# A Flamingo-style block on Trainium2: query projection moved into the cross attention stage, output bias on GpSimd, tanh kept in PSUM, one layer norm as a stage of its own

## What is computed

```
x = x + tanh(g_xattn[l]) * attention_l(layernorm(x), ctx)    # 16 heads of 16; 112 queries, 375 keys
x = x + tanh(g_ffn[l])   * ffn_l(layernorm(x))
```

```
h = gelu(x @ Wi + bi) * sigmoid(x @ Wg + bg);  r = x + h @ Wo + bo;  layernorm(r) * gamma + beta
```

## Time and profile before

| | |
|---|---|
| time, median of 2 runs | 3081.41 us (3079.08 to 3083.74) |
| the profiled execution | 3072.57 us |
| its span, first to last instruction | 3070.7 us |
| busy: PE, DVE, ACT, POOL | 85%, 60%, 44%, 34% of the span |
| mean granted PE clock | 0.917 of full |

### The profile page before, as it was taken

How to read it: one execution, slowest core, us unless ns; L and a number is a source line. 1 busy time by engine, 2 the same in 40 slices (tenths; PEclk the granted TensorE clock), 3 DMA queues, 4 the chain that set the end, 5 groups by cost and what they waited for, 6 DMA issues and landing times. The chain is left out here.

```text
span 3070.7 us, 57383 instructions
## 1 busy us (share of the span) xinstructions
PE 2604.8 (85%) x21112; PEld 2028.9 (66%) x21112; DVE 1848.1 (60%) x3903; ACT 1360.1 (44%) x2680; POOL 1057.2 (34%) x1305
## 2 busy tenths in 40 slices
PE   7998599986998999869599897977768994999995
PEld 7998387874876666546277563554445873888884
DVE  5555687136864333258478346678648865676775
ACT  4444466234662111247366423344334662455552
POOL 3433201022011232257412232453341113677772
PEclk9999699986998999989699998988987995999998
DMA  8888655327640000161655200000035723555553
GB/s 226 248 243 241 175 166 146 128 72 190 175 142 16 1 1 1 44 168 38 166 151 172 83 1 1 1 1 0 1 111 154 187 77 124 197 203 201 187 195 105
DMA packets 153095, 363.52 MB, mean 118 GB/s; under 512 B 26496, under 2 KB 110336, under 8 KB 137136
## 3 DMA queue, kind: packets, MB, share of 16 engines
q1 hardware_dynamic: 141120, 275.13, 31.5%
q0 software_dynamic: 11760, 85.51, 7.9%
HBM read 271.43 MB, written 88.67 MB: 117 GB/s over the span
## 5 line engine op out<-in xcount | busy, mean ns | idle before, releaser
L1030 ACT ACTIVATE arena<-ps 125x448 f32<-125x448 f32 x768 | 404.4, 544 | 312.3 <-PE ps L939 308.6
L1063 DVE TENSOR_REDUCE arena<-ps 112x2 f32<-112x750 f32 x384 | 348.1, 930 | 74.2 <-PE ps L923 69.0
L468 POOL TENSOR_SCALAR ln_var<-ln_mv 112x1 f32<-112x1 f32 x160 | 38.5, 240 | 933.5 <-DVE ln_mv L462 929.9
L923 PE MATMUL ps<-wreg,arena 96*112 96x375 bf16 x768 | 217.3, 372 | 79.7 <-DMA arena<-query_parts 50.9
L2723 PE MATMUL ps<-moe_x_r,moe_w_r 128*128 128x256 f32 x2016 | 256.1, 287 | 18.5 <-DVE arena L2875 17.1
L2723 PEld LDWEIGHTS ps<-moe_x_r,moe_w_r 128*128 128x128 f32 x2016 | 247.9, 193 | 23.8 <-DVE arena L2875 19.9
L939 PEld LDWEIGHTS ps<-arena,wreg 98*125 98x125 bf16 x2304 | 214.5, 142 | 60.8 <-issue 18.9
L939 PE MATMUL ps<-arena,wreg 98*125 98x112 bf16 x2304 | 236.3, 227 | 3.7 <-ACT arena L1030 2.9
L949 PE MATMUL ps<-arena 125*17 125x112 f32 x6144 | 199.8, 264 | 0.6 <-ACT arena L1030 0.6
L2289 POOL TENSOR_TENSOR arena<-arena 112x1024 f32<-112x1024 f32 x64 | 120.9, 1904 | 198.3 <-DVE arena L2412 155.1
L395 POOL TENSOR_TENSOR arena<-arena 128x375 bf16<-128x375 f32 x128 | 113.9, 913 | 186.3 <-ACT arena L338 186.3
(11 more groups left out here) (337 smaller groups left out, 5779.9 us busy)
## 6 DMA issues: line engine op xcount, KB each, us to landing
wreg<-key_parts SPq DMA_DIRECT2D x288, 187.5 KB, 3.9
key_parts<-arena SPq DMA_DIRECT2D x128, 281.2 KB, 3.9
arena<-query_parts SPq DMA_DIRECT2D x108, 224.0 KB, 4.6
values<-arena SPq DMA_DIRECT2D x64, 357.0 KB
arena<-values SPq DMA_DIRECT2D x64, 357.0 KB
arena<-key_parts SPq DMA_DIRECT2D x96, 187.5 KB, 3.7
query_parts<-arena SPq DMA_DIRECT2D x48, 336.0 KB, 2.5
wreg<-in_e_w SPq DMA_DIRECT2D x16, 704.0 KB, 5.4
```

Source lines behind the costliest of these rows:

```text
L923: mm = pe.matmul(ps[0:T, 2 * (p % 2) + e, 0:S2], queries(b)[0:SROWS, hd, :], keys[r][0:SROWS, hd, :], start=True, stop=True)
L1030: act.activation(probs[k % PROBS], ps[0:KN, 4 + k % 2, 0:GT], ACT.Exp, scale=scale).then_inc(at_probs, 1)
L1063: dve.tensor_reduce(negmax[r % 2][:, 2 * p:2 * p + 2], ps[0:T, 2 * (p % 2):2 * (p % 2) + 2, 0:S2], AX.X, ALU.max, negate=True).then_inc(at ...
```

## The change

- `query_stage` and `cross_stage` become one stage for the four cross attentions (class `Queries`); only the self attention keeps a `query_stage`. SP reads the first group's queries back when that group is stored, while the others are still being made. Loops over groups are written out.
- Keys of batches 0 and 1 (in layer 3 of batch 0, then the masks) are loaded ahead of the queries, the others later.
- The output bias goes from DVE to POOL, in 16 pieces, one per batch; DVE waits for a batch's piece before it adds that batch.
- All four buffers' ones are set by POOL, as pairs in float32 words (3000 words for 6000 halves). Two come before POOL's part of the queries, two behind it.
- `position_experts_stage` loses its woven norm; a `norm_stage` follows it.
- In the routed stage tanh is written in place in PSUM, `gelu` has four buffers, and ACT waits for DVE only four slices back.

```
+            def project(self, pe):
+                pe.wait_ge(loaded, self.ready)
+                for g in range(G):
+                    pe.wait_ge(ln_evac, self.turned + (g + 1) * GB)
+                    for j in range(self.tiles):
+                        at_least(pe, part_res, self.q0 + g * self.tiles + j - 1)
...
+            def piece(self, eng, q):
+                n = B // self.pieces
+                eng.tensor_tensor(self.dest[:, q * n:q * n + n, :], self.dest[:, q * n:q * n + n, :],
+                                  self.row.unsqueeze(1).broadcast_to([T, n, D]), ALU.add).then_inc(bias_added, 1)
...
             def sync(sp):
...
+                q.load(sp)
+                load_keys(sp, keys[0], kv, 0, 0)
+                if masked:
+                    for b in range(RING - 1):
+                        load_masks(b, b)
+                else:
+                    load_keys(sp, keys[1], kv, 1, 1)
+                q.store(sp, 0)
+                q.stored(sp, 0)
                 load_queries(0, range(len(Q_PART)))
...
+                q.store(sp, 1)
+                load_keys(sp, keys[1 + (not masked)], kv, 1 + (not masked), 1 + (not masked))
+                for g in range(2, G):
+                    q.store(sp, g)
+                load_values(0, 0)
...
+            def ones(eng, r):
+
+                eng.memset(keys[r][SROWS:AROWS, :, :].rearrange("p h k -> p (h k)").bitcast(F32), PAIR_OF_ONES).then_inc(const_made, 1)
+
             def gpsimd(pool):
+                pool.wait_ge(ln_ready, rows_scaled)
                 for r in range(2):
-                    pool.memset(keys[r][SROWS:AROWS, :, :], 1.0).then_inc(const_made, 1)
+                    ones(pool, r)
+                pool.wait_ge(const_made, ones_made - 2)
+                pool.wait_ge(loaded, q.ready)
+                q.low(pool)
...
+                for r in range(2, RING):
+                    ones(pool, r)
+                pool.wait_ge(const_made, ones_made)
+                out.bias.scale(pool)
+                for b in range(BIAS_AHEAD):
+                    out.bias.piece(pool, b)
                 for b in range(B + 6):
                     if 5 <= b < B + 5:
                         norm.deviation(pool, b - 5)
...
+                    if BIAS_AHEAD <= b < B:
+                        out.bias.piece(pool, b)
...
             def scalar(act):
+                q.high_and_middle(act)
                 act.activation(idle[:, :], one[:, :], ACT.Exp)
-
-
-                for r in range(2, RING):
-                    act.activation(keys[r][SROWS:AROWS, :, :], one[SROWS:AROWS, :].unsqueeze(2).broadcast_to([2, H, S2]), ACT.Copy).then_inc(const_made, 1)
...
             def vector(dve):
                 dve.memset(ps[:, SUMS, :], 0.0)
-                out.add_bias(dve)
+                q.remainders(dve)
...
-            gelu = [arena.take(128, BS) for _ in range(2)]
-            tanh = [arena.take(128, BS) for _ in range(2)]
+            GELUS = 4
+            gelu = [arena.take(128, BS) for _ in range(GELUS)]
...
-                        at_least(act, m_act, n - 1)
-                        act.activation(gelu[f % 2], ps[:, f % 4, 0:BS], ACT.Gelu, bias=bcols[u][:, 0, f:f + 1])
-
-                        act.activation(tanh[f % 2], ps[:, f % 4, BS:2 * BS], ACT.Tanh, scale=0.5, bias=half_b[u][:, f:f + 1]).then_inc(m_gate, 1)
+                        at_least(act, m_act, n - GELUS + 1)
+                        act.activation(gelu[f % GELUS], ps[:, f % 4, 0:BS], ACT.Gelu, bias=bcols[u][:, 0, f:f + 1])
+
+                        act.activation(ps[:, f % 4, BS:2 * BS], ps[:, f % 4, BS:2 * BS], ACT.Tanh, scale=0.5,
+                                       bias=half_b[u][:, f:f + 1]).then_inc(m_gate, 1)
...
             norm_stage(x, 1e-5)
-            w = query_stage(0, 1, x, gates[0:T, 0:1], keys_of=0)
             weights = PositionWeights()
-            cross_stage(0, w, 0.25, x, gates[0:T, 0:1], dict(eps=1e-5), weights.load_ahead)
-            position_experts_stage(4, weights, dict(eps=1e-5))
-
-            w = query_stage(1, 1, x, gates[0:T, 1:2], keys_of=1)
+            cross_stage(0, 0, 0.25, x, gates[0:T, 0:1], dict(eps=1e-5), weights.load_ahead)
+            position_experts_stage(4, weights)
+
+            norm_stage(x, 1e-5)
```

More of the change, by code:

```diff
@@ new lines, in query_stage @@
+        def query_stage(s, kinds):
+            arena.clear()
+            parts = [arena.take(128, DC * kinds, PARTS, GT, dtype=BF16) for _ in range(G)]
+            q = Queries(s, kinds, parts, [arena.take(128, GT) for _ in range(G * DC * kinds)])
+            def sync(sp):
+                q.load(sp)
+                for g in range(G):
+                    q.store(sp, g)
+                q.stored(sp, G - 1)
+            stage(sync, q.low, q.high_and_middle, q.remainders, q.project)
+            return q.w
@@ new lines, in build, with __init__, scale, whole @@
+        bias_scaled, bias_added = sem("bias_scaled"), sem("bias_added")
+        bias_count = {"scaled": 0, "added": 0}
+        BIAS_AHEAD = 5
+        class Bias:
+            def __init__(self, dest, gate, row, factors=None, pieces=2):
+                self.dest, self.gate, self.row, self.pieces = dest, gate, row, pieces
+                self.scaled = row if factors is None else factors
+                self.k, self.at = bias_count["scaled"], bias_count["added"]
+                bias_count["scaled"] += 1
+                bias_count["added"] += pieces
+                self.normed, self.stored = ln_at["normed"], ln_at["stored"]
+            def scale(self, eng):
+                eng.tensor_scalar(self.scaled, self.scaled, self.gate, None, ALU.mult).then_inc(bias_scaled, 1)
+                eng.wait_ge(bias_scaled, self.k + 1)
+                eng.wait_ge(ln_normed, self.normed)
+                at_least(eng, ln_stored, self.stored)
+            def piece(self, eng, q):
+                n = B // self.pieces
+                eng.tensor_tensor(self.dest[:, q * n:q * n + n, :], self.dest[:, q * n:q * n + n, :],
+                                  self.row.unsqueeze(1).broadcast_to([T, n, D]), ALU.add).then_inc(bias_added, 1)
+            def whole(self, eng):
+                self.scale(eng)
+                for q in range(self.pieces):
+                    self.piece(eng, q)
+            def done(self, eng, b=None):
+                eng.wait_ge(bias_added, self.at + (self.pieces if b is None or not isinstance(b, int) else b * self.pieces // B + 1))
@@ L762, in add @@
             def add(self, dve, n, b):
-                if not isinstance(b, int) or b == 0:
-                    dve.wait_ge(bias_added, self.biased)
+                self.bias.done(dve, b)
                 dve.wait_ge(o_made, n + 1)
@@ L821, in cross_stage @@
             vals = [arena.take(KN, KC, H, VW) for _ in range(RING)]
+            rows_scaled = ln_at["ready"]
+            shared = arena.at
             probs = [arena.take(KN, GT) for _ in range(PROBS)]
-            out = Output(w, dest, gate)
+            wlow.clear()
+            out = Output(wlow.take(128, 4, DC, D), dest, gate, B)
+            words = DC * PARTS * GT // 2
+            assert shared + (G - 1) * words <= arena.at
+            wreg.at, kept = KEPT_FREE_W, arena.at
+            arena.at = shared
+            parts = [arena.take(128, DC, PARTS, GT, dtype=BF16) for _ in range(G - 1)] + [wreg.take(128, DC, PARTS, GT, dtype=BF16)]
+            arena.at = kept
+            q = Queries(s, 1, parts, [wreg.take(128, GT) for _ in range(4)])
+            wreg.at = KEPT_FREE_W
             norm = RowNorm(dest, **norm)
@@ L846, in sync @@
             def sync(sp):
-                norm.load(sp)
                 def load_masks(b, r):
@@ L1346, in vector @@
                 dve.memset(ps[:, SUMS, :], 0.0).then_inc(const_made, 1)
-                out.add_bias(dve)
+                out.bias.whole(dve)
                 for u in range(2):
@@ L1450, in position_experts_stage @@
             rows = F0_ROWS
-            norm = RowNorm(x, **norm)
-            slots = [ps[:, 6 + u, 0:DC * T] for u in range(2)]
-            LAG = 4
             def experts(eng, step):
@@ L1523, in scalar @@
                 experts(act, step)
-                for b in range(B + 1):
-                    if b < B:
-                        norm.apply(act, b)
-                    if b > 0:
-                        norm.evacuate(act, b - 1, slots[(b - 1) % 2])
-            def gpsimd(pool):
-                for b in range(B):
-                    norm.deviation(pool, b)
             def vector(dve):
```

225 lines of the change are left out of this document (96 added, 129 removed).

## The result

| | before | after |
|---|---|---|
| time, median of 2 runs | 3081.41 us | 2997.23 us (2993.17 to 3001.29) |
| profiled execution, span | 3072.57, 3070.7 us | 2993.17, 2991.4 us |

The ratio is 0.9727, with an interval of 0.9662 to 0.9792: faster. I set the two profiled executions against each other at fixed points of the program; the gain up to a point is the difference of the starts.

A forecast was written before the change was run, and what follows sets the result against it. PE bounds the running attentions and nearly the routed stage; savings lie at the attention starts. Starts 52.8 - memsets 5.2 + routed stage 14 = 61.6 us, 3019.8 off the median 3081.4, given as 3019; range 2998 to 3042.

The forecast's parts named there:

- I take 4 of the 17.1: Routed stage: of PE's 17.1 us wait at slice 4, for slice 0's product, 4 us would go; stage sum 14 us.
- rival 1: Everything out of the way, 25%: DVE keeps POOL's memsets out and both routed PE waits go; 79.5 us saved, 3002.
- the upper bound: Routed stage: PE's idle ending with DVE's product, 17.1 + 10.2 = 27.3 us, is all this stage can give.
- I take one, 2.6 us per layer: Layers 0 and 1: one POOL memset delays DVE's 16 scalings; 5.2 us lost for both, bounds 0.6 and 10.4.
- Rival 2: POOL in the way, 22%: both memsets fall between the scalings, routed stage gives only 8 us; 50.4 saved, 3031.
- 0.85 us a batch: Layer 1, position experts' tail without its norm: a batch added every 0.85 us, 16 additions ending at 678.4.
- The norm by itself is nearly even: Layer 1: moving the norm out brings the first query split only 2.8 us earlier; earlier query weights are what pays.
- The early read: Attention starts: loads wait only for the first group's stores, 8.5 us from load to first pair; four starts save 52.8 us.
- Layer 3's first maximum: Layer 3's start: first maximum at 2298.5, after three penalties on DVE, against 2313.55 before; 15.0 us saved.
- The bias on POOL at nothing: Cross attentions: bias on POOL costs nothing; on DVE some 10 us per attention with the query load gone.
- The stall's move to L2839: Routed stage: the product's stall stays, moving to DVE's own weight split, which meets the same three POOL splits.
- rival 4: Routed stage, 3%: tanh in place in PSUM becomes the bound; with 1.5 us more per tanh, slower at 3104.

The follow-up runs named there:

- after_again: The changed kernel run again unedited, as base for edits of it: 0.9730 of the kernel before.
- r_both: The kernel before with only the change's routed stage (tanh in place in PSUM, four gelu buffers, ACT four slices ahead): 0.9902 of the kernel before.
- late_read: The changed kernel with the first group's queries read back only behind all four groups' stores, still without a meeting: 0.9908 of the kernel before.
- bias_dve: The changed kernel with the output bias back on DVE, in 16 pieces ahead of the first maximum: 0.9788 of the kernel before.
- norm_apart: The kernel before with only the norm taken out of the position experts' tail into a norm stage behind it: 0.9976 of the kernel before.

## Why the prediction was just outside

**Routed stage: the term that failed.** "I take 4 of the 17.1" for the wait at slice 4. In the changed kernel it went nearly whole (2.9 us left; 2.6 in `after_again`), in `r_both`, `late_read` and `bias_dve` by half (7.9 to 8.4 left). The prediction knew that the wait stands behind L2871 and that this instruction missed POOL's split by 0.13 us, and named it as rival 1 at 25%; but it took a value between two outcomes for what is a race with a sharp edge. DVE's tail had to get ahead of POOL's split by a few tenths of a microsecond only, and `r_both` shows the same instruction on either side of the edge from block to block. The second error there is the upper bound: 27.3 us, the idle time in the rows, was called all that the stage can give. It gave 31.1, since a wait costs PE more than the idle shown (0.69 us for one of 0.42). With 31 for 27 the range would have begun at 2994 and held the time. With 31.1 in place of 14 the same sum off the median gives 3081.4 - 78.7 = 3002.7, inside the range. The last 5 us are no step of mine: the profiled executions differ by 79.3 us and the medians of two runs each by 84.2. On which side of 2998 the time fell is luck: five more runs of the changed kernel, at 0.9730, would make it 2998.2.

**The memsets.** "I take one, 2.6 us per layer": both came in, 4.6 us per layer, 9.1 for both where 5.2 stood. Rival 2 had this right, and its reason was the better one: what an engine with a row of ready instructions does against the other was shown by L2875 against POOL's three in a row, not by the single L694. Here the row was DVE's, and it did not keep POOL out.

**The tail.** 0.85 us a batch was read from rows in which only the norm's turning and deviation were out of the way; DVE's own statistics of each batch were still between the additions. Without them it is 0.50, 5.3 us in favour, and `norm_apart` shows 8.6 us in all for the edit where 2.8 stood. "The norm by itself is nearly even" was wrong by that.

**What held.** The early read: 8.0 us from load to pair for 8.5, and 49 us lost when it is undone, where the four starts were put at 52.8. Layer 3's first maximum, its penalties and all. The bias on POOL at nothing that these runs can tell; but its price on DVE was 4 us per attention, not 10, since DVE has 3 us to spare and the pieces go at 0.39 us. The stall's move to L2839. Tanh took 446 ns in place in PSUM, so rival 4 did not come. Of ACT the page "ScalarE: Activation LUTs" of the Trainium skill says, in "Step-by-step: what each stage is for", that it reaches PSUM sooner than SBUF; the trace agrees, tanh takes 446 ns in place in PSUM and took 481 into SBUF.

**What a memset holds up.** L556 has one SBUF input and was held up by the memsets for 10.58 - 6.06 = 4.5 us; its first was held though it is recorded 0.02 us ahead of its memset. L709 has two and ran through beside them at 0.41 us each; what held up its first one, 1.13 us, was L666, which reads SBUF. The Trainium skill ("SBUF — State Buffer", Who interferes with whom) says of this: a DVE instruction with two SBUF inputs contends with a GpSimd instruction that reads SBUF, not with one that only writes it, while a two-port mode contends with every one. The trace agrees for L709; that L556 runs in a two-port mode no row shows, alone it takes 0.41 us for 256 columns, as L709 does. By that rule the choice of DVE's instruction decides what a memset beside it costs.

Rival 1's time, 3002 off the median, is nearest to what came, for half its reasons: both PE waits went, the memsets did not keep out, and the tail made up for them.

## What to carry to other kernels

Where two engines meet at an instruction by a tenth of a microsecond, forecast the two sides with their chances, not the middle; the edge decides a whole wait per round of the loop. A wait of PE cost more here than its idle row, so idle rows are no upper bound on what their removal gives. And a memset that is not needed soon belongs behind work that others wait for, not at the first moment at which its engine is free; what it meets at its new place is to be looked up too, here DVE's clamp.

## What was not expected of the hardware

DVE's back-to-back row of 16 one-input scalings let both of POOL's memsets in at its start (the first is recorded 0.02 us after it), while three of POOL's weight splits in a row kept DVE out for their whole 3.78 us: in both meetings POOL had its way. A single L2870 that began 0.08 us ahead of a split did keep it out (0.69 us for DVE, 1.76 for POOL). And the four running attentions before the change take 767 to 786 us in sum in different executions and on different chips; in some of them the granted clock falls to its lower level for some microseconds in the middle, behind a wait of PE of 1.25 to 2.8 us.
